# A gated attention and mixture-of-experts kernel on one core: the order of its opening is rewritten

## The reference, cut to what matters

```python
# x: 4 x 512 x 512, ctx_512: 4 x 512 x 128; 2048 tokens in all
# cross term: adj is layernorm(x), D = 128
si = einsum('bnd,d->bn', ctx, W[:, :D]); sj = einsum('bnd,d->bn', ctx, W[:, D:])
att = 0.6 * sigmoid(si[:, :, None] + sj[:, None, :] + b) + 0.4 * layernorm(x)
x = x + tanh(g_xattn) * att
# mixture of experts: E = 16, top 4, H = 512, I = 384, 4-bit weights with a scale per group of 128
h = layernorm(x)
probs = softmax(h @ gate_w.T); vals, idx = top_k(probs, 4); w = vals / sum(vals)
out  = sum over experts of combine * (swiglu(h @ dequant(gate_up[e])) @ dequant(down[e]))
out += swiglu(h @ dequant(shared_gate_up)) @ dequant(shared_down)
x = x + tanh(g_ffn) * out
```

## Time and profile before

| | us |
|---|---|
| median of 3 runs | 688.03 |
| lowest and highest | 687.14, 691.67 |
| the profiled execution, its time | 687.41 |
| the profiled execution, its span in the trace | 685.6 |
| TensorE busy | 629.7 (92%) |
| VectorE busy | 488.1 (71%) |
| GpSimd busy | 326.2 (48%) |
| ScalarE busy | 325.3 (47%) |

### The profile page before, as it was taken

How to read it: one execution, slowest core, us unless ns; L and a number is a source line. 1 busy time by engine, 2 the same in 40 slices (tenths; PEclk the granted TensorE clock), 3 DMA queues, 4 the chain that set the end, 5 groups by cost and what they waited for, 6 DMA issues and landing times.

```text
span 685.6 us, 17258 instructions
## 1 busy us (share of the span) xinstructions
PE 629.7 (92%) x4394; PEld 382.1 (56%) x4395; DVE 488.1 (71%) x1271; ACT 325.3 (47%) x558; POOL 326.2 (48%) x506
## 2 busy tenths in 40 slices
PE   3768969999998999999999999999999999999992
PEld 2444536557554656565665656566565656656561
DVE  6979779895766858588888767778588878767110
ACT  1763567331343455454544554454554545455541
POOL 3621834100334465564646555464655656565432
PEclk9999989999999999999999999999999999999997
DMA  8780101128157875768587594847767587654533
GB/s 234 202 247 2 63 31 64 62 54 276 49 172 160 189 173 127 176 123 195 110 203 176 126 223 74 226 85 201 168 135 183 117 199 158 152 86 77 93 39 39
DMA packets 49841, 93.72 MB, mean 137 GB/s; under 512 B 8840, under 2 KB 16776, under 8 KB 49816
## 3 DMA queue, kind: packets, MB, share of 16 engines
q0 software_dynamic: 16128, 38.35, 30.3%
q1 hardware_dynamic: 32936, 55.04, 27.5%
q10 hardware_dynamic: 752, 0.04, 0.1%
HBM read 65.16 MB, written 28.24 MB: 136 GB/s over the span
## 4 chain that ended last, share of the span: by engine, by line
PE 80%; DVE 6%; DMA 3%; ACT 3%; POOL 3%; issue 2%; SPq 1%; DVEq 0%; POOLq 0%; ACTq 0%
PE gu_ps L1207 45%; PE bank L1235 22%; PE bank L1247 4%; PE bank L1221 4%; DMA dn_sc<-dn_scale_halves 2%; PE bank L1262 1%; DMA room_a<-in_ctx 1%; PE gu_ps L1167 1%; POOL room_a L462 1%; PE bank L1164 1%; PE bank L1191 1%; DVE stats L725 1%; POOL X L445 1%; DVE X L1000 1%; ACT mix_room L581 1%
## 5 line engine op out<-in xcount | busy, mean ns | idle before, releaser
L1207 PE MATMUL gu_ps<-wgu,mix_room 128*128 x1728 | 305.9, 327 | 2.7 <-DVE tick L950 1.6
L1207 PEld LDWEIGHTS gu_ps<-wgu,mix_room 128*128 128x128 f16 x1728 | 166.5, 98 | 114.7 <-issue 7.5
L1235 PE MATMUL bank<-wdn,aT 128*128 (+1 forms) x792 | 186.2, 380 | 3.2 <-ACT aT L629 2.6
L530 POOL DMA_INDIRECT out<-mix_room,idx_s x72 | 122.9, 1707 | 32.4 <-issue 30.9
L629 ACT ACTIVATE aT<-bank 128x768 f16<-128x768 f16 x88 | 71.2, 809 | 139.5 <-PE bank L1221 136.2
L1235 PEld LDWEIGHTS bank<-wdn,aT 128*128 128x128 f16 x792 | 77.6, 98 | 88.8 <-issue 3.6
L501 POOL TENSOR_TENSOR pool_tick<-ones 128x1 f32<-128x1 f32 x144 | 35.7, 248 | 163.6 <-DMA out<-mix_room,idx_s 84.0
L991 DVE SCALAR_TENSOR_TENSOR act<-gu_ps,wslot,sg x72 | 44.5, 618 | 96.4 <-ACT sg L615 84.8
L622 ACT ACTIVATE acth<-act 128x384 f16<-128x384 f32 x88 | 46.0, 523 | 120.1 <-DVE act L991 120.1
L512 POOL DMA_INDIRECT room_b<-token_rows,idx_g x72 | 76.0, 1055 | 12.3 <-issue 3.6
L927 DVE TENSOR_TENSOR wgu<-dq_code,gu_sc 128x768 f16<-128x768 f16 x136 | 72.5, 574 | 2.3
(11 more groups left out here) (157 smaller groups left out, 588.1 us busy)
## 6 DMA issues: line engine op xcount, KB each, us to landing
dn_sc<-dn_scale_halves SPq DMA_DIRECT2D x34, 384.0 KB
dn_raw<-in_L_ffn_down_packed SPq DMA_DIRECT2D x48, 256.0 KB
gu_sc<-gu_scale_halves SPq DMA_DIRECT2D x34, 192.0 KB
X<-in_x SPq DMA_DIRECT2D x4, 1024.0 KB, 8.4
token_rows<-room_a SPq DMA_DIRECT2D x16, 256.0 KB, 2.2
out<-X SPq DMA_DIRECT2D x4, 1024.0 KB, 11.1
gu_raw<-in_L_ffn_gate_up_packed SPq DMA_DIRECT2D x16, 192.0 KB
gu_raw<-in_L_ffn_gate_up_packed SPq DMA_DIRECT2D x16, 191.9 KB
```

Source lines behind the costliest of these rows:

```text
L530: nc.gpsimd.indirect_dma_start(out[:, :], bass.IndirectOffsetOnAxis(idx_s[:, b:b + 1], 0), y_sb[:, b, :], None, compute_op=ALU.add).then_i ...
L1207: mm = nc.tensor.matmul(ps[b][:, 0:I], x(xp * HC + c), wgu[:, w, wp, c, col:col + I], start=(c == 0 and xp == 0 and wp == 0), stop=(c == H ...
L1235: mm = nc.tensor.matmul(y_ps[0 if shared else b][:, :], aT[:, b, ap, t, :], wdn[:, w, wp, t, :], start=(n == 0), stop=(n == 3 * IC - 1))
```

## The change

SyncE first loads only the shared expert's scales and its gate words, and splits, stores and reads back only those; X of batch 1, the other scales, X of batches 2 and 3 and expert 0's words follow. The split of the 16 experts' scales moves to VectorE's place behind shared slot 2, and SyncE stores them after the first four row tiles. ScalarE issues the contexts and the first X, around its six small loads. GpSimd finishes batch 0's second norm and low halves before it begins batch 1. VectorE, ScalarE and TensorE take the steps in another order; TensorE starts the first gate and up matmuls after one transposed x tile, not four. The scratch for the halves gets a place of its own (`sc_h`), and `LEAD`, a row of tiny memsets at the start of VectorE, goes from 64 to 58.

```diff
-        sc_cut = [0, SC_SH, SC_SH * NE, SC_SH * NE + SD_SH, (SC_SH + SD_SH) * NE]
+        sc_cut = [0, SC_SH, SC_SH + SD_SH, SC_SH * NE + SD_SH, (SC_SH + SD_SH) * NE]
...
-        LEAD = 64
+        LEAD = 58
...
-            load_ctx(0)
-            load_x(0)
-            for b in range(1, B):
-                load_ctx(b)
-            load_x(1)
-
-            sp.wait_ge(vs, SPLIT_STEPS)
...
-            sp.wait_ge(st_sc_sh, 64)
-            load_scales(sp, 0, 0)
-            sp.wait_ge(ld_w[0], 16 * LOADS)
-            for b in range(2, B):
-                load_x(b)
-            load_words(sp, gu_packed[0], dn_packed[0], 1)
-            sp.wait_ge(st_sc, 64)
-            load_scales(sp, 1, 1)
-            for i in range(NT):
...
+            load_scale_columns(0, sh_gu_scales.rearrange("g n -> (g n)"), ld_sc_sh)
+            load_scale_columns(1, sh_dn_scales.rearrange("g n -> (g n)"), ld_sc_sh)
+            load_gate_words(sp, sh_gu_packed, 0, ld_first)
+            sp.wait_ge(split_ready, 1)
+            store_scale_halves(0, st_sc_sh)
+            sp.wait_ge(st_sc_sh, 64)
+            load_gate_scales(sp, 0, 0, ld_first)
+            load_down_words(sp, sh_dn_packed, 0)
+            load_down_scales(sp, 0, 0)
+            load_x(1)
+            load_scale_columns(2, gu_scales.rearrange("e g n -> (e g n)"), ld_sc)
+            load_scale_columns(3, dn_scales.rearrange("e g n -> (e g n)"), ld_sc)
+            for b in range(2, B):
+                load_x(b)
+            load_words(sp, gu_packed[0], dn_packed[0], 1)
+            for i in range(TB):
+                store_rows(i)
+            sp.wait_ge(split_ready, 2)
+            store_scale_halves(1, st_sc)
+            sp.wait_ge(st_sc, 64)
+            load_scales(sp, 1, 1)
+            for i in range(TB, NT):
+                store_rows(i)
@@ gpsimd
             scaled_x(0)
-            inverse_std(0, 1)
-            scaled_x(1)
             inverse_std(1, 0)
             norm_factors(0)
             low_halves_x(0)
+            inverse_std(0, 1)
+            scaled_x(1)
             inverse_std(1, 1)
@@ scalar
+            load_ctx(0)
             for k in range(2):
                 a.dma_start(wij[:, k:k + 1], xattn_w.rearrange("o (k p) -> k p o", p=P)[k],
...
             a.dma_start(gws[:, :], gate_w).then_inc(ld_const, 16)
+            a.dma_start(X[:, 0:TB, :], x_t[0]).then_inc(ld_x[0], 16)
+            for b in range(1, B):
+                load_ctx(b)
...
-            for b in range(B - 1):
-                copy_ctxT(b)
-            scores(0)
-            copy_ctxT(B - 1)
-            scores(1)
+            copy_ctxT(0)
             for hl in range(2):
...
+            copy_ctxT(1)
+            scores(0)
+            copy_ctxT(2)
+            scores(1)
+            copy_ctxT(3)
             scores(2)
+            high_x(0)
+            high_x(1)
             scores(3)
-            for i in range(TB):
-                high_x(i)
-                if i:
-                    copy_xT(i - 1)
-            copy_xT(TB - 1)
+            copy_xT(0)
+            high_x(2)
+            copy_xT(1)
+            high_x(3)
...
-            for i in range(2):
-                activate(i, i)
+            activate(0, 0)
+            copy_xT(2)
+            activate(1, 1)
             copy_aT(0, 0)
             for i in range(2, NT):
                 copy_aT(i - 1, (i - 1) % 2)
+                if i == 2:
+                    copy_xT(3)
@@ vector
-            v.wait_ge(ld_sc, 64)
...
+            v.wait_ge(ld_sc_sh, 32)
+            split_scales(slice(0, sc_cut[2]))
...
+            split_gates()
             first_stats(0)
             row_scores(0)
-            split_gates()
             x_factors(0)
-            first_stats(1)
             row_scores(1)
             attend(0)
-            x_factors(1)
+            second_stats(0)
             row_scores(2)
-            second_stats(0)
-            row_scores(3)
             take_words(0, 0)
             for k in range(PARTS):
                 dequant(0, 0, k, None)
+                if k == 0:
+                    row_scores(3)
             v.wait_ge(dqs, 1 + PARTS * G_STEPS)
             nc.vector.memset(tick[:, 0:1], 0.0).then_inc(dqg_ready, 1)
+            first_stats(1)
...
                 if k == 0:
+                    take_words(1, 1)
                     dequant(1, 1, 0, None)
...
                 if i == 2:
+                    v.wait_ge(ld_sc, 32)
+                    split_scales(slice(sc_cut[2], SCW))
                     first_stats(2)
                     first_stats(3)
...
+            v.wait_ge(ld_w[0], loaded(0, 0))
             for d in range(PARTS):
                 if d % 2 == 0:
                     dequant(0, 0, None, d)
+                    if d == 0:
+                        x_factors(1)
...
             nc.vector.memset(tick[:, 0:1], 0.0).then_inc(dq_ready, 1)
-            take_words(1, 1)
             attend(1)
@@ tensor
             transpose_ctx(0)
-            transpose_ctx(1)
             pe.wait_ge(wj_ready, 1)
             pe.wait_ge(ld_const, 16 * 6)
             score_parts(0)
-            transpose_ctx(2)
-            score_parts(1)
-            transpose_ctx(3)
-            score_parts(2)
-            score_parts(3)
...
+            split_gate_weights()
+            for b in range(1, B):
+                transpose_ctx(b)
+                score_parts(b)
...
             pe.wait_ge(si_ready, B)
-            for i in range(TB):
-                transpose_x(i)
-                if i:
-                    route(i - 1)
+            transpose_x(0)
             pe.wait_ge(sig_ready, NT)
             pe.wait_ge(dqg_ready, 1)
-            for i in range(2):
-                for half in range(2):
-                    shared_gate_up(i, half)
-            route(TB - 1)
+            shared_gate_up(0, 0)
+            transpose_x(1)
+            route(0)
+            shared_gate_up(0, 1)
+            shared_gate_up(1, 0)
+            transpose_x(2)
+            route(1)
+            shared_gate_up(1, 1)
             transpose_act(0, 0)
...
                 transpose_act(i - 1, 1 - b)
+                if i == 2:
+                    transpose_x(3)
+                    route(2)
+                if i in WITH_X and i > 3:
+                    transpose_x(2 * i - 2)
                 if i in WITH_X:
-                    transpose_x(2 * i - 2)
-                if i in WITH_X and i > 3:
                     route(2 * i - 3)
...
                 shared_gate_up(i, 1)
+                if i == 3:
+                    transpose_x(2 * i - 2)
                 down(i - 1, 1 - b, 0)
```

More of the change, by code:

```diff
@@ L323, in gated_xattn_moe, with loaded @@
         LOADS = 2 + 2 + IC + 2
-        def loaded(n):
-            return 16 * LOADS * (n // 2 + 1)
+        FIRST_LOADS = 4
+        def loaded(n, buf):
+            return 16 * LOADS * (n // 2 + 1) - (16 * FIRST_LOADS if buf == 0 else 0)
         POOL_CONST = 15
-        LEAD = 64
+        LEAD = 58
         lead = sb("lead", [P, LEAD], F16)
         WITH_X = range(3, NT // 2 + 1)
-        SPLIT_STEPS = 5
         @block.sync
@@ L344, in spread, with load_scale_columns, store_scale_halves @@
                 return ap.rearrange("(p n) -> p n", n=sc_cut[k + 1] - sc_cut[k])
[L345 to L349 removed]
+            def load_scale_columns(k, ap, landed):
+                sp.dma_start(sc_all[:, columns(k)], spread(ap, k)).then_inc(landed, 16)
             def load_x(b):
                 sp.dma_start(X[:, b * TB:(b + 1) * TB, :], x_t[b]).then_inc(ld_x[b], 16)
[L353 to L361 removed]
+            def store_scale_halves(part, done):
+                for k, dram in ((2 * part, gu_s_dram), (2 * part + 1, dn_s_dram)):
                     for hl in range(2):
@@ L942, in take_words @@
                     v.wait_ge(dqs, n * N_STEPS + 1 - D_STEPS - 1)
-                v.wait_ge(ld_w[buf], loaded(n))
+                if isinstance(n, int) and n == 0:
+                    v.wait_ge(ld_first, 16 * FIRST_LOADS)
+                else:
+                    v.wait_ge(ld_w[buf], loaded(n, buf))
                 words = gu_raw[:, buf, :].bitcast(U16).rearrange("p (n f) -> p n f", f=2)
@@ L1167, in score_parts, with split_gate_weights @@
                 nc.tensor.matmul(sj_ps[b][:, :], wj_all[:, :], ctxT[:, b, :], start=True, stop=True).then_inc(sj_ready, 1)
+            def split_gate_weights():
+                pe.wait_ge(gw_ready, 1)
+                for hl in range(2):
+                    dst = tp_ps[hl][:, 0:HC * E // 2].bitcast(F16)
+                    for c in range(HC):
+                        mm = nc.tensor.transpose(dst[:, c * E:(c + 1) * E], chunk_h(gw_hl[:, hl, :], c), id16[0:E, 0:E])
+                    mm.then_inc(gwT_ps_ready, 1)
+                pe.wait_ge(gwT_ready, 2)
             transpose_ctx(0)
-            transpose_ctx(1)
             pe.wait_ge(wj_ready, 1)
@@ L1172, in _ @@
             score_parts(0)
-            transpose_ctx(2)
-            score_parts(1)
-            transpose_ctx(3)
```

(13 more changed lines are left out.)

44 lines of the change are left out of this document (26 added, 18 removed).

## The result

The changed kernel took 692.69 us (median of 20 runs, 688.67 to 695.29) beside 688.53 for the kernel before on the same chip (20 runs, 686.56 to 692.73): a ratio of 1.0055, 95% interval 1.0038 to 1.0072. It is slower by about half a per cent, some 4 us, where 687.5 was forecast and 691.5 was the upper end. Its profiled execution took 692.14 for a span of 690.3; before, 687.41 for 685.6.

What follows compares the result with a forecast made beforehand. It took the first 100 us as a four-engine relay carried mostly by VectorE. Factors of batches 2 and 3 at 77.0 against 77.21 gave -0.2, later costs +0.1: 687.41 became 687.3, named 687.5; range 682.5 to 691.5.

Steps and rivals of the forecast that it cites:

- the 1.1 of waiting for the last si: Opening: VectorE waits after the first gate part for the last si (27.7 against 26.7), 1.1 us with the bias.
- So: 2.4 for it: TensorE's first half of gate matmuls, beginning at 38.6, takes 2.4 us, ahead of the chain to `x_factors(1)`.
- the stall of 3.0: VectorE's new wait at `x_factors(1)` for GpSimd's power for batch 1, which stands behind batch 0's low halves: 3.0 us.
- rival (b): TensorE's clock drops at the stall before `dq_ready`; twelve and nine large matmuls run slowly, costing 2 us: 689.4; chance 0.11.
- down part 1.9: VectorE's down part after it leaves `x_factors(1)`, before the first product, takes 1.9 us as before.
- the 14.1 of the gate parts: VectorE's words and four gate parts took 14.1 us before, with three GpSimd low halves beside them, as again expected.
- All 612 took 3.5 ... so 3.3 now: Slot 2: VectorE's split of the other 576 of 612 scale columns takes 3.3 us, two of them hidden in idle time.
- Rival (a): Opening: ScalarE is held by its own DMA queue, scores start up to 2.3 us later; 689.6 at worst; chance 0.15.
- (c): Stall at `x_factors(1)` mostly absent, TensorE gains too: 3.0 and about 1 us, 683.3; chance 0.17 within 1%, 0.08 beyond.
- (d): Opening: read-back or last si comes so late that gate matmuls still start near 45; 693.8; chance 0.04.

Runs made afterwards that it cites:

- keep_clock: The changed kernel plus nine float32 score matmuls, results unread, on TensorE before the first gate half; ratio 1.0035 to the kernel before.
- down_parts_first: The changed kernel with three of the shared expert's down parts dequantized on VectorE ahead of `x_factors(1)`; ratio 0.9982 to the kernel before.
- before_late_split: The kernel before, with the experts' scales loaded later, split in slot 2 and stored late, without the new opening; ratio 1.0028 to the kernel before.
- first_two: The changed kernel, experts' split moved ahead of `x_factors(1)` and GpSimd's power and scaling of batch 1 before the last low half; ratio 1.0013 to before.
- norm_before_last_low: The changed kernel with GpSimd's power and scaling of batch 1 ahead of batch 0's last low half; ratio 0.9981 to the kernel before.

## Why the prediction was wrong

The order of events was forecast rightly: ScalarE free at 7.0 (7.32), first score at 9.4 (9.48), `take_words` at 23.4 (24.75), the signal at 38.6 (39.01), a new wait at `x_factors(1)` released by L464, five rows of a split in slot 2, no idle time left ahead of the third product. Three terms of the sum were too small: the first gate half, the down part and the split.

| point | forecast | measured | later than forecast by |
|---|---|---|---|
| gate weights signalled | 38.6 | 39.01 | 0.4 |
| VectorE leaves `x_factors(1)` | 47.5 | 49.35 | 1.9 |
| first product (behind one down part) | 49.4 | 52.49 | 3.1 |
| second tick | 56.5 | 59.55 | 3.1 |
| split begins | 65.0 | 67.94 | 2.9 |
| split ends | 68.3 | 72.87 | 4.6 |
| statistics end, third product | 74.9 | 78.87 | 4.0 |
| factors | 77.0 | 80.55 | 3.6 |

That the signal came within 0.4 of its forecast is luck in part. `take_words` was 1.4 late, for the last tile of batch 0's attention waited for GpSimd's scaling and ended at 21.6 and not at 20.0; and the 1.1 of waiting for the last si, which the sum held against it, did not come, for that si was made by 25.2 and not at 27.7 (batches 2 and 3 took their eight si matmuls in 1.05 us, where batch 0 had taken 1.84). ScalarE issued eleven transfers, not ten.

**"So: 2.4 for it", the first gate half.** It took 4.00. I took the 0.18 us a matmul of the 48 before, but before them TensorE had just done four tiles of transposes and router matmuls (from 37.03 to 45); in the new order it did one tile at 30.59 and then nothing for 7.57 us. keep_clock shows it: 2.11 with other matmuls in that gap. It is the larger part of why the stall of 3.0 became one of 4.89. The prediction had the slow clock as rival (b), but only for the later stall; the argument it gave against, that the first 48 were fast, was exactly what the change took away.

**"down part 1.9".** It took 3.14 (49.35 to 52.49) beside GpSimd's `scaled_x(1)`, which started as soon as the factors were there. The 1.9 came from a row with GpSimd idle beside it. That this step is the slow one in the change and the fourth part in down_parts_first speaks for the overlap as the cause; no run removed the overlap alone. The prediction knew of such an overlap, for it left three low halves in the 14.1 of the gate parts, and did not ask for one here or at the split.

**"All 612 took 3.5 ... so 3.3 now", the split.** It took 4.93 beside GpSimd's low halves, where before_late_split and first_two took 3.3. The row of the old split came from a time when GpSimd had nothing to do. The step itself was rightly placed, and 2.0 of it were rightly hidden.

The first makes 1.5 of the 1.9 in the second line of the table (the signal the other 0.4), the second 1.2, the third 1.6. Of their sum 0.2 is lost again before the split, 0.6 comes back because the statistics took 6.0 and not 6.6 (a step of 0.70 in the old rows, beside a low half, was counted in), and 0.4 between product and factors. So the factors are 3.6 later than forecast and 3.3 later than before, and the ratio says 3.8 us (2.6 to 5.0). The range was too narrow for a plain reason: each of the three was a duration read from a row of another neighbourhood, and I gave bounds to the opening's transfers but to none of these.

Rival (a), ScalarE held by its queue, did not happen; (c) and (d) neither. Of (b) one half did: the 12 gate matmuls at 54.72 took 3.63 us where 2.11 was usual, the nine down matmuls at 59.85 did not slow, and the 1.51 that TensorE was idle between them covers the loss. That the change would give back its lead was in the forecast; the runs price it. Without the wait (norm_before_last_low, down_parts_first) the change is 0.2% faster than before, at the edge of what these intervals tell from nothing. Taken with before_late_split, the account is: 3.7 us won at the signal, some 5 lost to the wait, 1 to 3 to the split, while the moved statistics of batch 1 (3.3) went for the most part into idle time that VectorE had before the first product (3.48). The account is put together from these runs; no single run measures all of its parts.

What stays open is why the last down matmuls of some profiled executions took 3.54 to 3.80 us and of others 2.11. It was not tried.

## What to carry to other kernels

When an engine is to start earlier, read what the others will do while it starts: a duration is that of its neighbourhood, so take it from a row with the same engine busy beside it, and bound it by the slow form where there is none. When a step is moved forward past others in one queue, look for a wait on it whose release has moved behind those others, and put work that needs nothing ahead of that wait; here one such edit of a few lines was worth about 5 us, where the new opening had won 3.7 at the gate weights' signal. And work that lay in another wait's shadow is no longer free when it is moved, even if it takes just as long.

## What the runs showed of the hardware

- The granted clock did not always tell that matmuls ran slow. The stretch from 28 to 44 us, which holds the first gate half, in the changed kernel and in down_parts_first (columns: stretch, length, VectorE busy, granted clock, DMA share, GB/s):

```profile
28.00:44.00 16.00, 15.26 (x35) 0.50 0.77 256
```

```profile
28.00:44.00 16.00, 15.04 (x34) 1.00 0.76 251
```

  One has the lower level (1.2 GHz), the other the full one (2.4), and the 12 matmuls took 4.00 and 3.69 us. So the slow first half is real in both, and it goes with TensorE's idle time before it; by the printed clock alone one would have missed it in the second. The durations are the safer reading.
- Three VectorE steps that started while a low half of GpSimd ran lengthened by nearly the same: 0.46 to 1.30 (`L749`), 0.76 to 1.60 (`L750`), 0.76 to 1.59 (`L747`). The low halves themselves took 1.16 us, and up to 1.44 beside them. Beside GpSimd's scaling of X the steps `L955`, `L961` and `L972` (two instructions) of a down part lengthened by 0.44 to 0.46. Not every step does: statistics beside the low halves kept their 2.46, and `L1033`, which reads from PSUM, kept its 0.60 beside the scaling.
- ScalarE was free of eleven DMA issues at 7.32 us; SyncE had been held 3.10 for three contexts, ScalarE was held 2.11 for the same three.
